# Sums of squares in the second cross-attention: from four columns to one row that a transfer spreads over the partitions

## The chip, the cores and the metric

The kernel runs on one core of one Trainium2 chip. The metric is the device time of one launch in microseconds; the kernel before takes 1813.54 us (median of three runs, 1813.4 to 1814.91).

## The reference

Four layers follow one another on x (8 x 256 tokens of 512 features), each added to x: a cross-attention, a feed-forward layer with ternary weights, a second cross-attention, and a mixture of experts. The change touches the second attention alone:

```
q = layernorm(x) @ Wq + bq        # 16 heads of 128
k, v = ctx @ Wk + bk, ctx @ Wv + bv   # 4 heads of 128, each serves 4 query heads
q = q * rsqrt(mean(q*q over the 128 of a head) + 1e-6) * qn_w     # RMS norm; k likewise
probs = softmax(q @ k.T / sqrt(128) + mask)
x = x + (probs @ v) @ Wo
```

For every token and head the kernel thus needs the sum of the squares of 128 values of q.

## The kernel before, in words

The program is written engine by engine, in an order set by hand; semaphores alone tie the engines together. Matrices in 32-bit precision are kept as two parts, `hi` and `lo`, and `matmul3` (L74 to L80) multiplies them with three matmuls.

The second attention (`ffn0_attention1`) works through 64 units, u = 0 to 63. A unit is one head for two of the eight batches (C = 512 tokens, CT = 4 tiles of 128). Four units (HG = 4) make a block; after the fourth, TensorE runs `project` (48 matmuls of 512 columns) for the four heads together, so each block has three short rounds and one long. There are four groups of query heads (G = 4) of 16 units each.

A query tile stands transposed: the head's 128 values on the partitions, the 512 tokens along the free axis. The steps of unit u, with the engine of each:

- `queries` (TensorE, 12 matmuls of 512 columns) gives q in one of two PSUM banks. ScalarE squares it into `sq` (L1360) and copies it into `q.hi` (L1361); VectorE writes `q.lo` (L1515).
- `square_sums` (TensorE, L1718): for each of the 4 tiles one matmul in full 32-bit precision, with the squares as the weights at rest and a column of ones moving. Its result stands as 128 x 4, a token on each partition. VectorE adds epsilon (L1520), GpSimd raises to the power -1/2 (L1224, `rstd`) and gives `rq`.
- `scores` (TensorE, 12 matmuls of 256 columns); VectorE scales them by `rq` and adds the mask (L1528), takes the negated maxima (L1535, `maxima`); ScalarE takes the exponentials (L1367, `exp`); VectorE divides (L1540, L1544, `normalise`).
- `transposed` (TensorE, L1750), split by ScalarE (L1373) and VectorE (L1549); `output` (TensorE, 12 matmuls of 256 columns on V), split by ScalarE (L1379) and VectorE (L1554).

The loop is a pipeline. In round u TensorE runs `transposed(u)`, `square_sums(u + 2)`, `queries(u + 3)`, `scores(u + 2)`, `output(u)` and, each fourth time, `project`. In the first round of a block `square_sums` stands ahead of `transposed`. In the first rounds of every second block ScalarE and GpSimd also split the next 2048-column weight tile (`wo_hi` and `wo_lo`, or `wq_hi` L1333 and `wq_lo` L1228), and in each block a key and a value tile (L1346 and L1241, L1351 and L1245).

Of the kernel before, what the change touches and what calls it, by code (L numbers as in the profile page):

```python
# [1010 lines left out]
def ffn0_attention1(nc, banks, X, eps, ident, ones, limit, W, keep, prep, stored, rstd, x1T_dram, ahead, first, wq1,  # L1011
# [24 lines left out]
    with Phase(nc) as ctx:  # L1036
# [20 lines left out]
        q = [over.pair(f"a1_q{j}", [P, C]) for j in range(2)]  # L1057
        sq = [over.take(f"a1_sq{j}", [P, C]) for j in range(2)]
# [10 lines left out]
        ssq = sb("ssq", [P, HG, CT])  # L1069
# [44 lines left out]
        s_sq, s_ssq, s_ssqc, s_rq = sema("q_squared"), sema("q_sum"), sema("q_sum_copied"), sema("q_rstd")  # L1114
# [322 lines left out]
        def _(dve):
# [185 lines left out]
            queries(2, 2)
            square_sums(1, 1)
# [29 lines left out]
        def _(pe):  # L1654
# [99 lines left out]
            def output(u):  # L1754
# [7 lines left out]
                for b in range(NB):  # L1762
# [1128 lines left out]
```

## Time and profile before

| | |
|---|---|
| median of three runs | 1813.54 us |
| the profiled execution | 1817.25 us, span 1815.5 us |
| granted TensorE clock | 0.985 of 2.4 GHz over the span |
| the 64 rounds of the second attention | from 651.0 us to about 1291 us |
| busy share of the span | PE 96%, DVE 67%, ACT 47%, POOL 32% |

PE is TensorE, DVE is VectorE, ACT is ScalarE, POOL is GpSimd, SP is SyncE. Times are counted from the first instruction of the span. Instructions of one engine overlap by some tens of nanoseconds, so the step from one start to the next is shorter than the duration that a row gives; an end of a matmul is modelled.

### The profile page before, as it was taken

The numbers are of one execution on the slowest core, as the hardware profiler recorded it, in microseconds if no ns is written. First come the engines' busy times: TensorE is split into PE (matmuls) and PEld (weight loads), VectorE is DVE, ScalarE is ACT, GpSimd is POOL, SyncE is SP. The second block draws the span as 40 slices with busy tenths as digits, with TensorE's granted clock in tenths as the row PEclk, the third lists the DMA queues.
The fourth block names the chain that finished last, engine by engine and source line by source line (L and its number), as shares of the span: only waits on it lengthen the run. The fifth ranks groups of instructions, "written<-read, shape, count | busy, mean of one in ns | idle before, by whom it ended". The sixth has DMA issues, their size and how long they took to land. (4 is left out here: it accounts for less than half of the span.)

```text
span 1815.5 us, 26738 instructions
## 1 busy us (share of the span) xinstructions
PE 1740.2 (96%) x9946; PEld 1443.8 (80%) x9966; DVE 1213.7 (67%) x2313; ACT 851.2 (47%) x1624; POOL 583.5 (32%) x441
## 2 busy tenths in 40 slices
PE   7999998996999989999999999999799999999998
PEld 6998997773444578888888888888667799999876
DVE  5444442895888777767777777777657567676555
ACT  4443432654565564445555555544341256566411
POOL 3111143224686531212132121211110245555342
PEclk9999998998999999999999999999899999999999
DMA  8323211853233761212232221110161488898573
GB/s 313 94 81 105 70 48 33 304 203 99 59 72 91 176 211 59 82 58 82 71 119 73 76 82 59 59 59 1 40 255 49 156 266 273 266 293 258 199 243 110
DMA packets 166346, 238.12 MB, mean 131 GB/s; under 512 B 42054, under 2 KB 103238, under 8 KB 164038
## 3 DMA queue, kind: packets, MB, share of 16 engines
q1 hardware_dynamic: 156620, 203.14, 34.4%
q0 software_dynamic: 9600, 33.30, 5.9%
q8 instruction: 80, 1.31, 0.3%
q14 instruction: 46, 0.38, 0.1%
HBM read 184.24 MB, written 43.78 MB: 126 GB/s over the span
## 5 line engine op out<-in xcount | busy, mean ns | idle before, releaser
L1224 POOL TENSOR_TENSOR a_rq<-a_ssq,a_qhalf 128x4 f32<-128x4 f32 x64 | 65.1, 1017 | 404.7 <-DVE a_ssq L1520 404.7
L1373 ACT ACTIVATE a_pT_hi<-bank 128x512 fp32r<-128x512 f32 x128 | 69.5, 599 | 186.1 <-PE bank L1750 185.9
L78 PE MATMUL bank<-a_xT_hi,a_wq_lo 128*128 128x512 f32 (+1 forms) x384 | 143.9, 375 | 1.4 <-DVE a_xT_lo L503 1.4
L1367 ACT ACTIVATE a_scores<-a_scores,a_nmax 128x256 f32<-128x256 f32 x256 | 127.2, 503 | 27.4 <-DVE a_nmax L1535 27.3
L80 PE MATMUL bank<-a_xT_hi,a_wq_hi 128*128 128x512 f32 (+1 forms) x384 | 138.3, 360 | 0.0
L79 PE MATMUL bank<-a_xT_lo,a_wq_hi 128*128 128x512 f32 (+1 forms) x384 | 138.1, 360 | 0.0
L78 PE MATMUL bank<-a_wo_hi,a_oT_lo 128*128 128x512 f32 x320 | 126.8, 396 | 2.9 <-DVE a_oT_lo L552 1.3
L2059 POOL TENSOR_TENSOR e_wg_lo<-raw_g,e_wg_hi 128x1408 fp32r<-128x1408 f32 x26 | 91.2, 3508 | 112.9 <-ACT e_wg_hi L2126 112.9
L1528 DVE SCALAR_TENSOR_TENSOR a_scores<-bank,a_rq,a_mask 128x256 f32<-128x256 f32 x256 | 106.1, 477 | 28.7 <-PE bank L80 20.4
L79 PE MATMUL bank<-a_wo_lo,a_oT_hi 128*128 128x512 f32 x320 | 124.9, 390 | 0.0
L80 PE MATMUL bank<-a_wo_hi,a_oT_hi 128*128 128x512 f32 x320 | 124.9, 390 | 0.0
L78 PE MATMUL bank<-a_pT_hi,a_V_lo 128*128 128x256 f32 x384 | 111.1, 289 | 8.1 <-DVE a_pT_lo L1549 6.3
L1260 POOL TENSOR_TENSOR f_h<-f_vv,f_gs 128x512 f32<-128x512 f32 x64 | 93.3, 1461 | 62.5 <-DVE f_vv L1465 61.8
L1560 DVE TENSOR_TENSOR X<-X,bank 128x512 f32<-128x512 f32 x64 | 43.8, 687 | 101.4 <-PE bank L80 101.4
L79 PE MATMUL bank<-a_pT_lo,a_V_hi 128*128 128x256 f32 x384 | 110.2, 287 | 0.0
L80 PE MATMUL bank<-a_pT_hi,a_V_hi 128*128 128x256 f32 x384 | 110.1, 287 | 0.0
L1549 DVE TENSOR_TENSOR a_pT_lo<-bank,a_pT_hi 128x512 fp32r<-128x512 f32 x128 | 82.1, 682 | 18.0 <-ACT a_pT_hi L1373 17.9
L1544 DVE TENSOR_SCALAR a_scores<-a_scores,a_rden 128x256 f32<-128x256 f32 x256 | 85.9, 399 | 2.3
L78 PEld LDWEIGHTS bank<-a_pT_hi,a_V_lo 128*128 128x128 f32 x384 | 75.1, 196 | 10.0 <-DVE a_oT_lo L1554 6.9
L80 PEld LDWEIGHTS bank<-a_xT_hi,a_wq_hi 128*128 128x128 f32 x384 | 73.7, 192 | 11.1
L78 PEld LDWEIGHTS bank<-a_xT_hi,a_wq_lo 128*128 128x128 f32 x384 | 74.1, 193 | 10.3 <-DVE a_xT_lo L503 1.8
L1535 DVE TENSOR_REDUCE a_nmax<-a_scores 128x2 f32<-128x512 f32 x128 | 81.2, 675 | 0.0
(416 smaller groups left out, 5326.2 us busy)
## 6 DMA issues: line engine op xcount, KB each, us to landing
raw_g<-in_egw SPq DMA_DIRECT2D x26, 704.0 KB, 4.7
raw_u<-in_euw SPq DMA_DIRECT2D x26, 704.0 KB, 6.2
a_xT_hi<-x1T_hi SPq DMA_DIRECT2D x16, 1024.0 KB, 6.1
a_xT_lo<-x1T_lo SPq DMA_DIRECT2D x16, 1024.0 KB, 8.5
raw_d<-in_edw SPq DMA_DIRECT2D x26, 512.0 KB, 5.9
y_routed<-m_y SPq DMA_DIRECT2D x39, 256.0 KB, 6.3
raw_d<-in_edw SPq DMA_DIRECT2D x26, 192.0 KB, 6.8
a_cTraw<-in_ctxT SPq DMA_DIRECT2D x8, 512.0 KB, 6.0
```

The lines of the kernel that those rows point to most:

```text
L78: pe.matmul(out, w[1], x[0], start=first, stop=False)
L79: pe.matmul(out, w[0], x[1], start=False, stop=False)
L80: return pe.matmul(out, w[0], x[0], start=False, stop=last)
L1224: pool.tensor_tensor(rq[:, h % HG, :], ssq[:, h % HG, :], qhalf[:], ALU.pow).then_inc(s_rq, 1)
L1260: pool.tensor_tensor(h[n % 2][:, j * 512:(j + 1) * 512], vv[u % 2][:], gs[u % 2][:], ALU.mult).then_inc(s_h, 1)
L1367: act.activation(row, row, ACT.Exp, bias=nmax[:, i % 2, t:t + 1], accum_out=den[:, i % 2, t:t + 1]).then_inc(s_exp, 1)
L1373: act.activation(pT[b].hi[:], ptb[b][:].rearrange("p (k s) -> p k s", k=QT), ACT.Copy).then_inc(ft.hi, 1)
L1528: dve.scalar_tensor_tensor(sc[i % 2][:, r, :], scb[b][:, t * S:(t + 1) * S], rq[:, i % HG, r:r + 1], mask[:, t, :], ALU.mult, ALU.add).the ...
L1535: dve.tensor_reduce(nmax[:, i % 2, b * QT:(b + 1) * QT], sc[i % 2][:, b * QT:(b + 1) * QT, :], AX.X, ALU.max, negate=True).then_inc(s_nmax, 1)
L1544: dve.tensor_scalar(row, row, rden[:, i % 2, t:t + 1], None, ALU.mult).then_inc(s_p, 1)
L1549: dve.tensor_tensor(pT[b].lo[:], ptb[b][:].rearrange("p (k s) -> p k s", k=QT), f32(pT[b].hi[:]), ALU.subtract).then_inc(ft.lo, 1)
L2059: pool.tensor_tensor(pairs[w % 2].g.lo[:], raws[raw_of(w)].g[:], f32(pairs[w % 2].g.hi[:]), ALU.subtract).then_inc(s_glo, 1)
```

## The change

Squares get the treatment of the other operands: `sq_hi` is a rounded copy of `sq` (ScalarE), `sq_lo` is the rest (VectorE). Now the ones rest in the array, as a single column `ones_r`, and the squares move, in two matmuls of 512 columns that add up in PSUM. The result is one row of 512 sums on partition 0. ScalarE copies that row to SBUF, adding epsilon and putting the four tiles' values of each token place side by side, and issues a transfer from its own queue that lays the row out as 128 x 4. GpSimd waits for that transfer.

The places in the order change with it. On TensorE `square_sums(u + 3)` now stands in round u between the two halves of `output(u)`, one unit further ahead than before. VectorE does `queries(u + 3)` and the new `squares(u + 3)` ahead of `scores(u + 2)`. ScalarE does `square_sums(u + 3)` (row copy and transfer) late in round u, ahead of its `output(u)`. The prologue is rearranged alike.

```diff
@@ scalar
             def queries(u, g, i, begin=False):
                 act.wait_ge(fq.mm, u + 1)
-                if not begin:
-                    act.wait_ge(s_ssq, u - 1)
...
+                after(act, s_ssq, u - 1)
                 act.activation(sq[i % 2][:], qb[i % 2][:], ACT.Square, bias=b).then_inc(s_sq, 1)
                 act.activation(q[i % 2].hi[:], qb[i % 2][:], ACT.Identity, bias=b).then_inc(fq.hi, 1)
+                after(act, s_ssq, u)
+                act.wait_ge(s_sq, u + 1)
+                act.activation(sq_hi[:], sq[i % 2][:], ACT.Copy).then_inc(s_sqhi, 1)
+
+            def square_sums(u):
+                act.wait_ge(s_ssq, u + 1)
+                if u:
+                    act.wait_ge(s_col[(u - 1) % 2], (u - 1) // 2 * 16 + 16)
+                act.activation(sum_row[0:1, :].rearrange("a (p t) -> a t p", t=CT),
+                               ssb[0:1, :].rearrange("a (t p) -> a t p", t=CT), ACT.Identity,
+                               bias=sum_eps[0:1, :]).then_inc(s_row, 1)
+                act.wait_ge(s_row, u + 1)
+                after(act, s_rq, u - 1)
+                act.dma_start(ssq[u % 2][:], sum_row[0:1, :].rearrange("a (p t) -> a p t", t=CT)).then_inc(s_col[u % 2], 16)
...
+                if u + 3 < G * U:
+                    square_sums(u + 3)
                 output(u, n, i)
@@ gpsimd
-                pool.wait_ge(s_ssqc, u + 1)
-                pool.tensor_tensor(rq[:, h % HG, :], ssq[:, h % HG, :], qhalf[:], ALU.pow).then_inc(s_rq, 1)
+                pool.wait_ge(s_col[u % 2], u // 2 * 16 + 16)
+                pool.tensor_tensor(rq[:, h % HG, :], ssq[u % 2][:], qhalf[:], ALU.pow).then_inc(s_rq, 1)
@@ vector
-            def square_sums(u, i):
-                dve.wait_ge(s_ssq, u + 1)
-                dve.tensor_scalar(ssq[:, i % HG, :], ssb[:, 0:CT], HD * RMS_EPS, None, ALU.add).then_inc(s_ssqc, 1)
+            def squares(u, i):
+                dve.wait_ge(s_sqhi, u + 1)
+                dve.tensor_tensor(sq_lo[i % 2][:], sq[i % 2][:], f32(sq_hi[:]), ALU.subtract).then_inc(s_sqlo, 1)
...
-                if u + 2 < G * U:
-                    square_sums(u + 2, i + 2)
                 transposed(u)
                 if u + 1 < G * U:
                     normalise(u + 1, i + 1)
+                if u + 3 < G * U:
+                    queries(u + 3, i + 3)
+                    squares(u + 3, i + 3)
                 if u + 2 < G * U:
                     scores(u + 2, i + 2)
-                if u + 3 < G * U:
-                    queries(u + 3, i + 3)
-                if u + 2 < G * U:
                     maxima(u + 2, i + 2)
@@ tensor
             def square_sums(u, i):
-                pe.wait_ge(s_sq, u + 1)
+                pe.wait_ge(s_sqlo, u + 1)
...
-                after(pe, s_ssqc, u)
-                for t in range(CT):
-                    last = pe.matmul(ssb[:, t:t + 1], sq[i % 2][:, t * P:(t + 1) * P], ones[:, 0:1], start=True,
-                                     stop=True)
-                last.then_inc(s_ssq, 1)
+                after(pe, s_row, u)
+                pe.matmul(ssb[0:1, :], ones_r[:], sq_hi[:], start=True, stop=False)
+                pe.matmul(ssb[0:1, :], ones_r[:], sq_lo[i % 2][:], start=False, stop=True).then_inc(s_ssq, 1)
...
-                if i % HG == 0 and u + 2 < G * U:
-                    square_sums(u + 2, i + 2)
                 transposed(u, n, i)
-                if i % HG and u + 2 < G * U:
-                    square_sums(u + 2, i + 2)
                 if u + 3 < G * U:
                     queries(u + 3)
                 if u + 2 < G * U:
                     scores(u + 2)
-                output(u)
+                output(u, range(1))
+                if u + 3 < G * U:
+                    square_sums(u + 3, i + 3)
+                output(u, range(1, NB))
```

TensorE, before, at the turn from one short round to the next (a_pT and a_V are `output`, ident is `transposed`, a_xT and a_wq are `queries`; each L1718 matmul in full 32-bit precision is two on the engine):

```order
L79 MATMUL bank<-a_pT_lo,a_V_hi 128x256
L80 MATMUL bank<-a_pT_hi,a_V_hi 128x256
L1750 MATMUL bank<-ident,a_scores_4403 128x128 x8
L1718 MATMUL bank<-ones,a_sq_4411 128x1 x4
L78 MATMUL bank<-a_xT_hi,a_wq_lo 128x512
```

TensorE, of the change, in the middle of `output(u)`:

```order
L78 MATMUL bank<-a_pT_hi,a_V_lo 128x256
L79 MATMUL bank<-a_pT_lo,a_V_hi 128x256
L80 MATMUL bank<-a_pT_hi,a_V_hi 128x256
L1746 MATMUL bank<-a_sq_hi,a_ones_r 1x512
L1747 MATMUL bank<-a_sq_lo_4410,a_ones_r 1x512
L78 MATMUL bank<-a_pT_hi,a_V_lo 128x256
L79 MATMUL bank<-a_pT_lo,a_V_hi 128x256
```

The sums stand later in the round than the matmuls whose result they square, with 18 matmuls of 256 columns between (12 of `scores`, 6 of `output`); before, a whole `output` and a `transposed` stood between.

VectorE, before, one short round:

```order
L1549 TENSOR_TENSOR a_pT_lo<-bank,a_pT_hi 128x512 x2
L1540 RECIPROCAL a_rden<-a_den 128x4
L1544 TENSOR_SCALAR a_scores_4402<-a_scores_4402,a_rden 128x256 x4
L1528 SCALAR_TENSOR_TENSOR a_scores_4403<-bank,a_rq,a_mask 128x256 x4
L1515 SCALAR_TENSOR_TENSOR a_q_lo<-bank,a_bqg,a_q_hi 128x512
L1535 TENSOR_REDUCE a_nmax<-a_scores_4403 128x2 x2
L1554 TENSOR_TENSOR a_oT_lo<-bank,a_oT_hi 128x512
```

VectorE, of the change, the same stretch:

```order
L1578 TENSOR_TENSOR a_pT_lo<-bank,a_pT_hi 128x512 x2
L1569 RECIPROCAL a_rden<-a_den 128x4
L1573 TENSOR_SCALAR a_scores_4402<-a_scores_4402,a_rden 128x256 x4
L1544 SCALAR_TENSOR_TENSOR a_q_lo<-bank,a_bqg,a_q_hi 128x512
L1549 TENSOR_TENSOR a_sq_lo_4410<-a_sq_4412,a_sq_hi 128x512
L1557 SCALAR_TENSOR_TENSOR a_scores_4403<-bank,a_rq,a_mask 128x256 x4
L1564 TENSOR_REDUCE a_nmax<-a_scores_4403 128x2 x2
```

`q_lo` and the new `sq_lo` now stand ahead of the scores.

ScalarE, of the change, one short round (before, L1372, L1378 and the DMA were not there):

```order
L1395 ACTIVATE a_pT_hi<-bank 128x512 x2
L1389 ACTIVATE a_scores_4403,a_den<-a_scores_4403,a_nmax 128x256 x4
L1368 ACTIVATE a_sq_4413<-bank,a_bqg 128x512
L1369 ACTIVATE a_q_hi<-bank,a_bqg 128x512
L1372 ACTIVATE a_sq_hi<-a_sq_4413 128x512
L1355 ACTIVATE a_K_hi<-ahead_ctx 128x512
L1378 ACTIVATE a_sum_row<-bank,a_sum_eps 1x4x128
L1383 DMA a_ssq_4428<-a_sum_row 128x1x4
L1401 ACTIVATE a_oT_hi<-bank 128x512
```

The row copy, which waits for TensorE's sums, and the transfer stand ahead of `a_oT_hi` and of everything of the next round.

## Rows read from the trace of the kernel before

**Rows 1.** The page, part 1: engine, busy us (share of the span), instructions.
```profile
PE 1740.2 (96%) x9946; PEld 1443.8 (80%) x9966; DVE 1213.7 (67%) x2313; ACT 851.2 (47%) x1624; POOL 583.5 (32%) x441
```
**Rows 2.** Windows of two blocks: length, busy by engine, PE clock, DMA.
```profile
900.12:941.33 41.21, 41.05 (x258) 36.55 (x257) 31.18 (x68) 22.12 (x56) 12.04 (x8) 1.00 0.27 90
941.33:982.38 41.05, 40.95 (x257) 36.51 (x256) 29.39 (x68) 20.72 (x54) 6.62 (x6) 1.00 0.19 65
```
**Rows 3.** Timeline of TensorE, first rounds of a block: start us, duration us, instruction.
```profile
941.33 1.09 PE L1750 MATMUL bank<-ident,a_scores 128*128 128x128 f32 x8
942.17 0.48 PE L78 MATMUL bank<-a_xT_hi,a_wq_lo 128*128 128x512 f32 x1
...
944.79 0.39 PE L80 MATMUL bank<-a_xT_hi,a_wq_hi 128*128 128x512 f32 x1
...
947.16 0.28 PE L78 MATMUL bank<-a_pT_hi,a_V_lo 128*128 128x256 f32 x1
...
947.89 1.03 PE L1750 MATMUL bank<-ident,a_scores 128*128 128x128 f32 x8
...
955.31 0.38 PE L1750 MATMUL bank<-ident,a_scores 128*128 128x128 f32 x2
```
**Rows 4.** Timeline of ScalarE in the same round.
```profile
942.99 0.51 ACT L1367 ACTIVATE a_scores<-a_scores,a_nmax 128x256 f32<-128x256 f32 x1
943.48 0.51 ACT L1367 ACTIVATE a_scores<-a_scores,a_nmax 128x256 f32<-128x256 f32 x1
...
945.21 0.69 ACT L1360 ACTIVATE a_sq<-bank,a_bqg 128x512 f32<-128x512 f32 x1 [0.15 <-PE bank L80]
945.80 0.68 ACT L1361 ACTIVATE a_q_hi<-bank,a_bqg 128x512 fp32r<-128x512 f32 x1
946.37 0.63 ACT L1346 ACTIVATE a_K_hi<-ahead_ctx 128x512 fp32r<-128x512 f32 x1
948.09 0.60 ACT L1379 ACTIVATE a_oT_hi<-bank 128x512 fp32r<-128x512 f32 x1 [1.08 <-PE bank L80]
948.58 1.08 ACT L1373 ACTIVATE a_pT_hi<-bank 128x512 fp32r<-128x512 f32 x2
```
**Rows 5.** Timeline of VectorE in the same round.
```profile
948.29 0.74 DVE L1515 SCALAR_TENSOR_TENSOR a_q_lo<-bank,a_bqg,a_q_hi 128x512 fp32r<-128x512 f32 x1
948.95 1.26 DVE L1535 TENSOR_REDUCE a_nmax<-a_scores 128x2 f32<-128x512 f32 x2
```
**Rows 6.** Single lines of the kernel: duration ns min/median/max, first and last start.
```profile
L486 DVE TENSOR_TENSOR a_wq_lo<-a_wraw,a_wq_hi x4: 682/684/686, 9.5 to 13.6; 128x512 fp32r<-128x512 f32 x4
L2151 ACT ACTIVATE r_lg<-bank x4: 586/586/587, 1320.8 to 1356.4; 16x512 f32<-16x512 f32 x4
L1224 POOL TENSOR_TENSOR a_rq<-a_ssq,a_qhalf x64: 1007/1008/1106, 637.7 to 1280.2; 128x4 f32<-128x4 f32 x64
L2587 PE MATMUL bank<-r_xT_lo,r_rw x16: 387/396/632, 1317.6 to 1356.0; 128*8 128x512 f32 x16
L1190 SPq DMA_DIRECT2D a_xT_lo<-x1T_lo x14: 627/632/1257, 657.8 to 1192.3; - x14
```
**Rows 7.** Timeline of SyncE's queue: start, issue duration.
```profile
1317.08 0.32 SPq L2023 DMA_DIRECT2D xT_hi<-r_xT_hi  x1
```
**Rows 8.** Transfers: KB each, us from issue to landing.
```profile
r_gbias<-in_egb SPq DMA_DIRECT2D x1, 3.0 KB, 2.6
a_xT_lo<-x1T_lo SPq DMA_DIRECT2D x16, 1024.0 KB, 8.5
```
**Rows 9.** Timeline of ScalarE, GpSimd, VectorE in a block with a weight tile.
```profile
905.18 1.92 ACT L1333 ACTIVATE a_wq_hi<-ahead_raw 128x2048 fp32r<-128x2048 f32 x1
907.18 4.62 POOL L1228 TENSOR_TENSOR a_wq_lo<-ahead_raw,a_wq_hi 128x2048 fp32r<-128x2048 f32 x1 [5.77 <-ACT a_wq_hi L1333]
912.92 1.30 POOL L1241 TENSOR_TENSOR a_K_lo<-ahead_ctx,a_K_hi 128x512 fp32r<-128x512 f32 x1
911.37 3.02 DVE L1544 TENSOR_SCALAR a_scores<-a_scores,a_rden 128x256 f32<-128x256 f32 x4
```

More of the change, by code:

```diff
@@ L1057, in ffn0_attention1 @@
         q = [over.pair(f"a1_q{j}", [P, C]) for j in range(2)]
+        sq_lo = Region(nc, over.offset)
+        sq_lo = [sq_lo.take(f"a1_sq_lo{j}", [P, C], F32R) for j in range(2)]
         sq = [over.take(f"a1_sq{j}", [P, C]) for j in range(2)]
@@ L1068, in ffn0_attention1 @@
         bqg = [first.bqg, sb("bqg", [P, HG])]
-        ssq = sb("ssq", [P, HG, CT])
+        ones_r, sum_eps = sb("ones_r", [P, 1], F32R), sb("sum_eps", [P, 1])
+        ssq = [sb(f"ssq{j}", [P, CT]) for j in range(2)]
         qhalf = sb("qhalf", [P, CT])
@@ L1086, in ffn0_attention1 @@
         wraw, xT, mask, bq = ahead.raw, first.xT, first.mask, first.bq
+        over = Region(nc, keep.gate_area)
+        sq_hi, sum_row = over.take("a1_sq_hi", [P, C], F32R), over.take("a1_sum_row", [P, C])
+        assert over.offset <= keep.gate_area + 2 * H
         gb, vb, x1b, fob, xb = banks[0:2], banks[2:4], banks[5], banks[4:8:2], banks[7][:].bitcast(BF16)
@@ L1113, in ffn0_attention1 @@
         fq, ft, fo = (Flow(ctx, nc, "a1_" + n) for n in ("q", "pT", "oT"))
-        s_sq, s_ssq, s_ssqc, s_rq = sema("q_squared"), sema("q_sum"), sema("q_sum_copied"), sema("q_rstd")
+        s_sq, s_sqhi, s_sqlo, s_ssq, s_row, s_rq = (sema(n) for n in (
+            "q_squared", "q_squared_hi", "q_squared_lo", "q_sum", "q_sum_row", "q_rstd"))
+        s_col = [sema(f"q_sum_column{j}") for j in range(2)]
         s_sc, s_masked, s_nmax, s_exp, s_rden, s_p = (sema(n) for n in (
@@ L1245, in values_lo @@
                 pool.tensor_tensor(V[n % 2].lo[:], first.Vraw, f32(V[n % 2].hi[:]), ALU.subtract).then_inc(s_vlo, 1)
+            pool.memset(sum_eps[:], HD * RMS_EPS).then_inc(s_const, 1)
             pool.memset(qhalf[:], -0.5).then_inc(s_const, 1)
             pool.memset(last.mhalf[:], -0.5).then_inc(s_lhalf, 1)
-            pool.wait_ge(s_const, 1)
+            pool.wait_ge(s_const, 2)
             pool.wait_ge(s_lhalf, 1)
@@ L1406, in _ @@
             next_norm(T - 4)
+            act.wait_ge(s_const, 2)
+            act.activation(ones_r[:], ones[:, 0:1], ACT.Copy).then_inc(s_const, 1)
             queries(0, 0, 0, True)
@@ L1409, in _ @@
             next_norm(T - 3)
+            square_sums(0)
             queries(1, 0, 1, True)
             next_hi(T - 3)
+            next_norm(T - 2)
+            square_sums(1)
             exp(0, 0)
-            next_norm(T - 2)
             queries(2, 0, 2)
@@ L1416, in _ @@
             next_norm(T - 1)
+            square_sums(2)
             next_hi(T - 1)
@@ L1611, in _ @@
             queries(0, 0)
+            squares(0, 0)
             next_lo(T - 4)
@@ L1614, in _ @@
             queries(1, 1)
+            squares(1, 1)
             ffn_add(T - 1)
@@ L1617, in _ @@
             next_mean(T - 1)
-            square_sums(0, 0)
+            next_lo(T - 3)
+            next_shift(T - 2)
             scores(0, 0)
             maxima(0, 0)
-            next_lo(T - 3)
-            next_shift(T - 2)
             queries(2, 2)
-            square_sums(1, 1)
+            squares(2, 2)
             next_lo(T - 2)
@@ L1752, in transposed, with output @@
                     last.then_inc(ft.mm, 1)
-            def output(u):
+            def output(u, halves):
                 i, n = u % U, u // HG
@@ L1761, in output @@
                 after(pe, fo.lo, u)
-                for b in range(NB):
+                for b in halves:
                     pe.wait_ge(ft.lo, u * NB + b + 1)
@@ L1766, in output @@
                                        part(pT[b], slice(None), k), k == 0, k == QT - 1)
-                last.then_inc(fo.mm, 1)
+                if NB - 1 in halves:
+                    last.then_inc(fo.mm, 1)
             def project(u, n):
@@ L1799, in _ @@
             queries(1, True)
+            square_sums(0, 0)
             down(T - 1)
-            square_sums(0, 0)
+            square_sums(1, 1)
             next_xT(T - 3)
@@ L1804, in _ @@
             queries(2)
-            square_sums(1, 1)
             next_xT(T - 2)
             scores(1)
+            square_sums(2, 2)
             next_xT(T - 1)
@@ L2794, in program @@
             keep.base = nc.sbuf_base
+            keep.gate_area = keep.base - 2 * H
             xT = [None, next_pair("a1_xT1", [P, KD, C], 1)]
```

1 line of the change is left out of this document (added).

## The prediction

> **What bounds the kernel now.** I read the page first: TensorE is busy 96% of the span [rows 1]. Then windows over two blocks of the second attention, cut where TensorE starts a block: 41.21 and 41.05 us long, TensorE busy for 41.05 and 40.95, VectorE for 31.2 and 29.4, ScalarE for 22.1 and 20.7, the clock at its upper level [rows 2]. TensorE idles for about 0.1 us in a block, so there is no slack in which a new wait on it could vanish: what it saves is gained in full and what it waits is lost in full. That holds only while the others keep up, so the timelines of the three engines in one round come next, to see when each result that the change makes TensorE wait for could be there.
>
> I count from 941.33, the start of a block's first round [rows 3]. TensorE starts its first query matmul at +0.84; the last starts at +3.46 and ends at +3.85; the second half of output(u) starts at +5.83, and the round is over at +6.56. This round holds no square sums (they stand ahead of it). The next one holds them and is 955.31 - 947.89 = 7.42 long, so the sums of one unit cost 0.86.
>
> **What TensorE saves.** The new sums are two matmuls of 512 moving columns with one column at rest. The steps of the queries give the price: 11 steps in 944.79 - 942.17 = 2.62, that is 0.24 each [rows 3]. That few resting columns make no odds is seen where eight rest: 387 to 396 ns for 512 columns, as the 390 of a query matmul [rows 3, 6]. So 0.47 in place of 0.86: 0.39 saved per unit, 64 x 0.39 = 25.0 us.
>
> **What TensorE waits.** The sums of u + 3 stand after the first half of output(u), thus at +5.83. They need sq_lo, and that has a chain behind it which starts when the last query matmul ends, at +3.85: ScalarE starts the squares at +3.88 and q_hi at +4.47, which ends at +5.15 [rows 4]; sq_hi follows at +5.04 and takes about what the copy in its place takes now (0.63, to +5.67), so it is not what is late. VectorE starts q_lo 0.04 after q_hi's end, at +5.19; a follower of it starts 0.66 later [rows 5], sq_lo at +5.85. A subtraction of two SBUF tiles of this shape takes 0.684 [rows 6]: +6.53, and with 0.04 for the semaphore TensorE goes on at +6.57. It wanted to at +5.83: a wait of 0.74. Nothing can shorten this in the first round of a block, where the other engines have caught up behind the projection. It is more than the 0.39 saved.
>
> In the rounds after, the chain is longer, since ScalarE has a loop. From the start of a unit's sums: both matmuls done +0.63 (0.24 + 0.39); semaphore 0.04; the row copy, one partition of 512 elements, which I take at the 0.59 of a 16-partition copy out of PSUM [rows 6]: +1.26; semaphore +1.30; the transfer's issue, d; then a_oT_hi 0.49, two pT_hi at 0.49, four exponentials at 0.49 with their accumulator reads (the step from 942.99 to 943.48), the squares 0.59, and q_hi to its end 0.68 [rows 4]: 1.30 + d + 0.49 + 0.98 + 1.96 + 0.59 + 0.68 = 6.00 + d; then as above 0.04, q_lo 0.66, sq_lo 0.68, semaphore 0.04: 7.42 + d from sums to sums. TensorE's own work in that time is 6.56 + 0.47 = 7.03. The wait is thus 0.39 + d, and at least 0.74. The key and value copies (0.57) don't lengthen the loop: they stand where ScalarE waits for the sums.
>
> The trace has no transfer issued by ScalarE. SyncE's take from 0.32 [rows 7] over 0.63 in the median to 1.26 [rows 6]. I take 0.5, since most stand at 0.3 to 0.65: a wait of 0.89. The Trainium skill (DMA: Bandwidth & Descriptors, Anatomy of one DMA — SWDGE (gpsimd) path) puts a sequencer's dispatch at about 50 ns, for GpSimd's kind of transfer; the issue rows here are six times that and more. By the page's figure every wait would be at its floor of 0.74, and the sum about 7 us lower.
>
> The loop issues sums for 61 units (three belong to the prologue): 16 first rounds at 0.74 = 11.8 and 45 others at 0.89 = 40.1, together 51.9 us.
>
> **Blocks with a weight tile.** In seven blocks (four wo tiles, three wq) the first round has ScalarE round a tile for 1.92, from 905.18 to 907.10 [rows 9]. Now sq_hi stands ahead of it and the row copy behind it: tile, bias and key copies end at about +8.0, while the sums are ready for the row copy at 6.57 + 0.67 = +7.2. The loop starts about 0.75 late, and TensorE waits that longer. Besides, four divisions of VectorE took 3.02 and ended at 914.39, just behind GpSimd's a_K_lo (912.92 + 1.30 = 914.22) [rows 9]; such a block has 1.8 more of VectorE's time than the other kind [rows 2]. Now TensorE pays nothing for that; after the change q_lo and sq_lo stand behind those divisions and TensorE behind sq_lo. So between 0.75 and 2.6 in each; I take 1.5, less than the middle, as the collision needs GpSimd to hit the same instructions: 7 x 1.5 = 10.5 us. The Trainium skill (SBUF — State Buffer, SBUF: two separate sides) says that a VectorE operation with two SBUF inputs and a GpSimd one that reads SBUF exclude each other for the whole instruction. The 3.02 agrees with such a lock; sq_lo has two SBUF inputs and so could be held up too, by the rule for up to 4.62 in a block. In my times it lies 1 us or more clear of GpSimd's long operation.
>
> **What stays hidden.** A transfer of 3 KB lands 2.6 after its issue [rows 8], which I take for this one of 2 KB; GpSimd's power takes 1.0 [rows 6]. So rq is there 1.8 + 2.6 + 1.1 = 5.5 after the sums began, and VectorE asks for it at 7.9: 2.4 to spare. VectorE gains 0.60 and loses 0.07 in a round; its 29.4 to 31.2 of 41 become 31.5 to 33.3, which is no bound. The epsilon add on VectorE goes off a path that was not limiting. The prologue has TensorE idle around these sums anyway, and its end hangs on layer norm copies: 0, give or take 2.
>
> **The sum.** -25.0 + 51.9 + 10.5 = +37.4 on the profiled execution of 1817.25 (span 1815.5): 1854.7. That execution is 3.7 over the median of the runs, so the median becomes 1813.5 + 37.4 = 1851.
>
> Ends: with d = 0.32 all waits at 0.74 (45.1) and 0.75 in seven blocks, +25, 1839. If sq_lo lands 0.08 earlier and the tiles cost nothing, 61 x 0.66 - 25.0 = +15, 1829. With d = 1.26 the 45 waits are 1.65: 86.1 - 25.0 + 7 x 2.6 = +79, 1893.
>
> **The rivals.** (1) Faster: the squares are ready when TensorE comes to them. The matmuls between the queries' end and the sums last 1.98 and the chain must then fit in; with no wait at all the 25 us of the saving remain: 1788. Point of decision: a wait under 0.39 per unit. For it stands only that VectorE and ScalarE have spare time overall; against it that each of the five steps has its own row, and that they sum to 2.7. 0.06; a wait near 0.39, no change, 0.04.
> (2) The row's transfer is late. The large loads of x take 8.5 to land [rows 8] and one starts in most blocks; if the little transfer queues behind it for, say, 8, rq comes 3 after VectorE asks, of which 1 is spare before the exponentials start: 2 x 14 blocks = +28 more, 1879. Against: it is 128 tiny pieces on another queue. 0.08.
> (3) An issue from ScalarE costs as SyncE's longest: 1893 with all its company, about 1882 with the tile blocks at 1.5. 0.08.
> My forecast, a wait at its 0.74 to 1.0: 0.74. Less than 0.2% (3.6 us) either way can't be told from no change here. Only rival 1 gives faster, 0.06; same 0.04; slower 0.90. Range 1829 to 1883: it leaves out rival 1, no change, and half of rival 3.
>
> **What would show it.** Right: TensorE idle before L1746 (the first of the two sums) for 0.7 to 1.0 in each round, released by VectorE's sq_lo L1549; two matmuls at 0.24 steps there; a plain block about 43 long in place of 41.05; ScalarE waiting for TensorE before L1378; rq waiting for nothing but its transfer, some 2 to 3 after issue; VectorE's scores not waiting for rq. Wrong: no idle before L1746 (rival 1), scores released by GpSimd's L1232 in most rounds (rival 2), a gap of over 1 between L1378 and the next ScalarE instruction (rival 3), or the sums' matmuls far from 0.24.

## The result and the profile after

The changed kernel takes 1915.3 us (median of 4 runs, 1909.47 to 1916.69) where the kernel before takes 1814.22 beside it (1813.4 to 1815.51): slower by 5.5%, ratio 1.0549 with a 95% interval of 1.0535 to 1.0564. The prediction was 1851, range 1829 to 1883. Its sign held and the two waits that it named were found; their sizes, and a third wait that it did not have, put the time outside the range: the profiled span went from 1815.5 to 1914.8, +99.3, where +37.4 was forecast. Of the kernels below, one of the four runs of E6 took 2857 us at a granted clock of 0.556 and is left out of its median and ratio.

Page, part 1, of after (answers to [rows 1]), and windows of two blocks of after, one without and one with a weight tile (columns as in [rows 2], which they answer to):

```profile
PE 1738.9 (91%) x9562; PEld 1411.3 (74%) x9582; DVE 1249.9 (65%) x2313; ACT 953.1 (50%) x1753; POOL 586.3 (31%) x442
```
```profile
990.58:1036.56 45.98, 39.96 (x232) 33.70 (x233) 31.78 (x68) 26.81 (x62) 7.02 (x6) 1.00 0.18 58
845.39:895.01 49.62, 42.27 (x233) 35.66 (x233) 33.52 (x68) 28.69 (x63) 12.02 (x8) 0.93 0.23 75
```

A plain block (one without a weight tile) took 41.05 before and one with a tile 41.21. In the plain block TensorE now works 1.0 us less than before (39.96 against 40.95) and idles 6.0, where it idled 0.1; in the other it is busy 1.2 longer, part of it at a lower clock, and idles 7.4. The 64 rounds, from the start of the first to that of the last, grew from 639.1 to 734.2: +95.1 of the +99.3. What stands ahead of them grew by 2.0, what follows by 2.2.

TensorE of after, first two rounds of the plain block that starts at T = 990.58 (answers to [rows 3]):

```profile
990.58 1.09 PE L1777 MATMUL bank<-ident,a_scores 128*128 128x128 f32 x8 [0.78 <-DVE X L1589]
...
997.17 0.40 PE L1746 MATMUL bank<-a_sq_hi,a_ones_r 128*1 128x512 f32 x1 [0.60 <-DVE a_sq_lo L1549]
...
997.40 0.40 PE L1747 MATMUL bank<-a_sq_lo,a_ones_r 128*1 128x512 f32 x1
...
998.35 1.03 PE L1777 MATMUL bank<-ident,a_scores 128*128 128x128 f32 x8
...
1005.86 0.39 PE L1746 MATMUL bank<-a_sq_hi,a_ones_r 128*1 128x512 f32 x1 [1.54 <-DVE a_sq_lo L1549]
```

ScalarE (answers to [rows 4]) and VectorE (to [rows 5]) of after in the same rounds:

```profile
994.46 0.69 ACT L1368 ACTIVATE a_sq<-bank,a_bqg 128x512 f32<-128x512 f32 x1 [0.16 <-PE bank L80]
995.05 0.68 ACT L1369 ACTIVATE a_q_hi<-bank,a_bqg 128x512 fp32r<-128x512 f32 x1
995.62 0.63 ACT L1372 ACTIVATE a_sq_hi<-a_sq 128x512 fp32r<-128x512 f32 x1
...
997.84 1.19 ACT L1378 ACTIVATE a_sum_row<-bank,a_sum_eps 1x512 f32<-1x512 f32 x1 [1.07 <-PE bank L1747]
...
999.05 0.48 ACTq L1383 DMA_DIRECT2D a_ssq<-a_sum_row  x1
...
999.63 0.60 ACT L1401 ACTIVATE a_oT_hi<-bank 128x512 fp32r<-128x512 f32 x1 [0.61 <-ACT a_sum_row L1378]
...
1003.04 0.69 ACT L1368 ACTIVATE a_sq<-bank,a_bqg 128x512 f32<-128x512 f32 x1
```
```profile
995.77 0.75 DVE L1544 SCALAR_TENSOR_TENSOR a_q_lo<-bank,a_bqg,a_q_hi 128x512 fp32r<-128x512 f32 x1
...
996.43 0.68 DVE L1549 TENSOR_TENSOR a_sq_lo<-a_sq,a_sq_hi 128x512 fp32r<-128x512 f32 x1
...
1004.46 0.75 DVE L1544 SCALAR_TENSOR_TENSOR a_q_lo<-bank,a_bqg,a_q_hi 128x512 fp32r<-128x512 f32 x1
...
1005.12 0.68 DVE L1549 TENSOR_TENSOR a_sq_lo<-a_sq,a_sq_hi 128x512 fp32r<-128x512 f32 x1
```

The first round is 998.35 - 990.58 = 7.77, which is 6.56 + 0.47 + 0.74 as forecast, with the sums at +6.59. From these sums to the next, though, is 1005.86 - 997.17 = 8.69, not 7.92. Step by step: the row copy starts at +0.67 (as forecast) and takes 1.21 to the transfer's issue (forecast 0.63 with its semaphore); the issue 0.58 to the next instruction (0.50); `a_oT_hi` to the next squares 3.41 (3.43); those to `q_lo` 1.42 (1.31); `sq_lo` 0.66 later, TensorE 0.74 behind that (0.72). Of the 0.77 too much 0.58 is the row copy. And the first line of TensorE's rows holds a wait that the forecast doesn't have: the block begins 0.78 late, behind VectorE's last add of the projection (L1589).

Waits of after, 640 to 1400 us (engine, line, waited for, us in total, times, longest), and its single lines L1378 and L1383, the latter also to landing:

```profile
POOL a_rq L1232 <- DMA a_ssq<-a_sum_row: 363.6, 58, 19.8
PE bank L1746 <- DVE a_sq_lo L1549: 90.4, 62, 4.1
ACT a_sum_row L1378 <- PE bank L1747: 88.8, 54, 3.1
```
```profile
L1378 ACT ACTIVATE a_sum_row<-bank,a_sum_eps x64: 1146/1191/1220, 632.6 to 1373.0; 1x512 f32<-1x512 f32 x64
```
```profile
L1383 ACTq DMA_DIRECT2D a_ssq<-a_sum_row x64: 477/477/545, 633.8 to 1374.2; - x64
...
DMA to landing us min/median/max: 1.9/2.0/6.1
```

Last the block with a weight tile: its rounds are 7.81, 11.80, 9.12 and 20.88, where the plain block's are 7.77, 8.70, 8.64 and 20.87. ScalarE, GpSimd, VectorE and TensorE in it (answers to [rows 9]):

```profile
851.00 1.91 ACT L1350 ACTIVATE a_wo_hi<-ahead_raw 128x2048 fp32r<-128x2048 f32 x1
...
853.32 1.18 ACT L1378 ACTIVATE a_sum_row<-bank,a_sum_eps 1x512 f32<-1x512 f32 x1
...
858.88 2.09 DVE L1573 TENSOR_SCALAR a_scores<-a_scores,a_rden 128x256 f32<-128x256 f32 x4
...
861.05 1.25 POOL L1253 TENSOR_TENSOR a_V_lo<-ahead_ctx,a_V_hi 128x512 fp32r<-128x512 f32 x1
861.55 1.31 DVE L1549 TENSOR_TENSOR a_sq_lo<-a_sq,a_sq_hi 128x512 fp32r<-128x512 f32 x1
...
862.91 0.59 PE L1746 MATMUL bank<-a_sq_hi,a_ones_r 128*1 128x512 f32 x1 [3.76 <-DVE a_sq_lo L1549]
```
```profile
858.00:862.00 4.00, 1.15 (x10) 0.95 (x8) 3.30 (x7) 2.82 (x8) 3.97 (x4) 0.89 0.58 197
862.00:866.00 4.00, 3.09 (x13) 2.69 (x14) 3.61 (x7) 1.49 (x2) 0.30 (x1) 0.50 0.59 200
866.00:870.00 4.00, 4.00 (x17) 3.38 (x16) 2.36 (x5) 3.35 (x11) 1.01 (x1) 0.76 0.02 1
```

`sq_lo` takes 1.31 instead of 0.68 and ends 0.56 behind GpSimd's `a_V_lo`; TensorE waits 3.76, from 859.15 to 862.91. The granted clock falls to 0.50, the lower level of 1.2 GHz, within that wait and stays there for the whole second window (the 0.89 and the 0.76 beside it are means over both levels). Between 650 and 1420 us after has nine stretches at the lower level, 64.9 us together, before four of 27.3.

Not every such wait was followed by the lower level. In the block that starts at T = 1132.21 TensorE waits as long:

```profile
1149.70 0.40 PE L1746 MATMUL bank<-a_sq_hi,a_ones_r 128*1 128x512 f32 x1 [3.74 <-DVE a_sq_lo L1549]
```
```profile
1132.21:1180.39 48.18, 39.94 (x232) 33.70 (x232) 33.25 (x68) 28.60 (x64) 11.99 (x8) 1.00 0.23 77
```

Its clock stays at 1.00, and it takes 48.18, which is 2.2 over a plain block, where four blocks with the lower level take 3.6 to 3.75 more than one.

### The profile page after: what moved, and what is told of

Its sections match the earlier page's. It is cut to its first block and busy times, and to the rows that moved or that the text cites. A ratio compares the mean times of both kernels' runs of the same rounds, so it can differ in the third digit from the quotient of the medians.

```text
span 1914.8 us, 26420 instructions
## 1 busy us (share of the span) xinstructions
PE 1738.9 (91%) x9562; PEld 1411.3 (74%) x9582; DVE 1249.9 (65%) x2313; ACT 953.1 (50%) x1753; POOL 586.3 (31%) x442
## 5 line engine op out<-in xcount | busy, mean ns | idle before, releaser
L1378 ACT ACTIVATE a_sum_row<-bank,a_sum_eps 1x512 f32<-1x512 f32 x64 | 76.2, 1190 | 88.8 <-PE bank L1747 88.8
L1589 DVE TENSOR_TENSOR X<-X,bank 128x512 f32<-128x512 f32 x64 | 43.7, 687 | 111.4 <-PE bank L80 111.4
L1269 POOL TENSOR_TENSOR f_h<-f_vv,f_gs 128x512 f32<-128x512 f32 x64 | 93.2, 1460 | 62.5 <-DVE f_vv L1494 61.8
L1746 PE MATMUL bank<-a_sq_hi,a_ones_r 128*1 128x512 f32 x64 | 25.9, 405 | 91.5 <-DVE a_sq_lo L1549 91.5
L1777 PE MATMUL bank<-ident,a_scores 128*128 128x128 f32 x512 | 74.4, 293 | 14.3 <-DVE X L1589 11.7
```

What stands on the lines that cost most here:

```text
L1269: pool.tensor_tensor(h[n % 2][:, j * 512:(j + 1) * 512], vv[u % 2][:], gs[u % 2][:], ALU.mult).then_inc(s_h, 1)
L1378: act.activation(sum_row[0:1, :].rearrange("a (p t) -> a t p", t=CT), ssb[0:1, :].rearrange("a (t p) -> a t p", t=CT), ACT.Identity, bias= ...
L1777: last = pe.transpose(ptb[b][:, k * S + t * P:k * S + (t + 1) * P], sc[i % 2][:, r, k * P:(k + 1) * P], ident[:])
```

## The experiments

All times are medians, and the kernel before took 1813.24 to 1813.85 beside those of E1 to E12. "Rounds" are the four of an undisturbed block without a weight tile, first to last, from one start of `transposed` to the next.

| kernel | us | against before (95%) | rounds | such a block |
|---|---|---|---|---|
| before | 1814.22 | | 6.56, 7.42, 7.4, 19.7 | 41.05 |
| after | 1915.3 | 1.0535 to 1.0564 | 7.77, 8.70, 8.64, 20.87 | 45.98 |
| E1 | 1901.59 | 1.0467 to 1.0502 | 7.77, 8.18, 8.12, 20.37 | 44.44 |
| E2 | 1898.8 | 1.0451 to 1.0496 | 7.77, 8.18, 8.12, 20.37 | 44.44 |
| E3 | 1898.86 | 1.0453 to 1.0488 | 7.06, 8.68, 8.64, 20.87 | 45.25 |
| E4 | 1895.44 | 1.0431 to 1.0470 | 8.37, 8.68, 8.65, 19.1 | 44.78 |
| E5 | 1905.13 | 1.0486 to 1.0527 | as after | 46.0 |
| E6 | 1845.62 | 1.0156 to 1.0206 | 6.56, 6.99, 6.98, 19.6 | 40.12 |
| E7 | 1903.79 | 1.0476 to 1.0511 | 7.86, 8.27, 8.21, 20.45 | 44.78 |
| E8 | 1828.08 | 1.0055 to 1.0093 | 7.45, 7.41, 7.40, 19.66 | 41.92 |
| E9 | 1814.86 | 0.9993 to 1.0014 | 6.56, 6.76, 6.84, 19.01 | 39.17 |
| E10 | 1810.61 | 0.9969 to 0.9991 | 6.78, 6.74, 6.74, 18.99 | 39.25 |
| E11 | 1833.21 | 1.0070 to 1.0110 | as E6 | 40.3 to 41.0 |
| E12 | 1805.75 | 0.9936 to 0.9968 | as E9 | 39.1 |

### E1, E2 and E7: the row copy

E1 writes the row in one run and leaves the tokens in the order of the tiles:

```diff
-                act.activation(sum_row[0:1, :].rearrange("a (p t) -> a t p", t=CT),
-                               ssb[0:1, :].rearrange("a (t p) -> a t p", t=CT), ACT.Identity,
-                               bias=sum_eps[0:1, :]).then_inc(s_row, 1)
+                act.activation(sum_row[0:1, :], ssb[0:1, :], ACT.Identity, bias=sum_eps[0:1, :]).then_inc(s_row, 1)
```

> The row copy writes its 512 values one behind the other, the transfer is the same; so the four sums of a token are not those of its four tiles, and the output is another. Theory A (ScalarE's loop of 8.69 us from sums to sums sets the rounds, and 0.6 of it is the price of writing in steps of 16 bytes): the copy takes 0.59 in place of 1.19, short rounds behind the first of a block go from 8.7 to 8.1, 45 x 0.6 = 27 us less, 1888 us (1883 to 1893). Theory B (the row costs 1.19 because a single partition is slow to copy): no change. Theory C (the transfer's landing sets the rounds): no change.

E2 keeps the order of after, and puts the steps on the side that is read (512 bytes apart in PSUM):

```diff
-                act.activation(sum_row[0:1, :].rearrange("a (p t) -> a t p", t=CT),
-                               ssb[0:1, :].rearrange("a (t p) -> a t p", t=CT), ACT.Identity,
+                act.activation(sum_row[0:1, :].rearrange("a (p t) -> a p t", t=CT),
+                               ssb[0:1, :].rearrange("a (t p) -> a p t", t=CT), ACT.Identity,
```

> The copy walks the tokens, reads PSUM in steps of 128 values and writes in one run. If only a write in steps is slow: 0.59 for the copy and 27 us less than the changed kernel, 1888 us. If a read in steps is as slow: 1.19 and 1915 us.

E7 copies as E1 and lets the matmuls read the squares in that order:

```diff
-                pe.matmul(ssb[0:1, :], ones_r[:], sq_hi[:], start=True, stop=False)
-                pe.matmul(ssb[0:1, :], ones_r[:], sq_lo[i % 2][:], start=False, stop=True).then_inc(s_ssq, 1)
+                turned = lambda x: x.rearrange("k (t p) -> k p t", t=CT)
+                pe.matmul(ssb[0:1, :], ones_r[:], turned(sq_hi[:]), start=True, stop=False)
+                pe.matmul(ssb[0:1, :], ones_r[:], turned(sq_lo[i % 2][:]), start=False, stop=True).then_inc(s_ssq, 1)
```

> The sums' matmuls read the squares in steps of 128 values, so that the row comes out in the right order and the copy runs through. If the matmul's step stays at 0.23: as e1, 1888 us. If a moving operand read in steps of 512 bytes is slower, say twice, two matmuls cost 0.46 more in each of 61 rounds: 1888 + 28 = 1916.

The row copy in E2, and the first matmul of the sums in E7 and in after, as single lines:

```profile
L1378 ACT ACTIVATE a_sum_row<-bank,a_sum_eps x64: 657/679/682, 628.7 to 1355.2; 1x512 f32<-1x512 f32 x64
```
```profile
L1745 PE MATMUL bank<-a_sq_hi,a_ones_r x64: 432/433/588, 631.5 to 1363.9; 128*1 128x512 f32 x64
```
```profile
L1746 PE MATMUL bank<-a_sq_hi,a_ones_r x64: 386/397/587, 631.9 to 1372.3; 128*1 128x512 f32 x64
```

The copy falls from 1.19 to 0.68, whether its read is in one run (E1, median 680 ns) or in steps (E2, 679). So the stepped write alone costs the 0.51, and each round behind it is 0.51 shorter (8.69 to 8.18): one for one on TensorE. The Trainium skill (SBUF — State Buffer, Door 1: The DMA port swizzle) says that each access to a new 16-byte line of SBUF pays a penalty. The write of after, in steps of 16 bytes, agrees with that. The same paragraph says that non-contiguous PSUM access slows matmuls; for ScalarE's read of PSUM no run here shows a cost, and the matmuls of E7 read their squares from SBUF. In E7 the stepped read costs 36 ns in a matmul and 0.09 in a round, far from twice the time, and the kernel came out between its two forecasts (1903.79).

The forecast for E1 and E2 was 27 us less, and they came out 13.7 and 16.5 less. The plain block gained 1.54, which over 15 blocks would be 23, but blocks with a weight tile gained next to nothing: six of the seven stayed at 49 to 50 us, as their second round grew from 11.8 to 12.7 in most of them, and the lower clock came in ten stretches of 61.4 us together.

### E3 and E4: another place for the sums

E3 puts them behind the whole `output(u)`:

```diff
-                output(u, range(1))
+                output(u, range(NB))
                 if u + 3 < G * U:
                     square_sums(u + 3, i + 3)
-                output(u, range(1, NB))
```

> The sums behind both halves of the output. Theory A (a chain that starts at the queries' end in a block's first round, then a loop of 8.69 on ScalarE): the first round's wait of 0.7 is filled by the second half, the loop of the others is as long as before, so a block gains 0.71 once: 16 x 0.71 = 11 us less, 1904 (1900 to 1908). Rival (each round's wait stands by itself and 0.71 of it is filled each time): 61 x 0.71 = 43 less, 1872.

The first round lost its wait (7.77 to 7.06), the other three none (8.70 to 8.68, 8.64, 20.87): they are held by the ring through ScalarE, from sums to sums, which TensorE's place for them doesn't shorten. E3 is 16.4 under after where 11 was forecast (range 1900 to 1908, measured 1898.86): the seven blocks with a tile came down by 8.4 together, and 7 x 0.71 is 5.0. E4 moves only the long round's sums, behind `project`, on TensorE and ScalarE:

```diff
@@ scalar
+                late = i % HG == HG - 1
-                if u + 3 < G * U:
+                if u + 3 < G * U and not late:
                     square_sums(u + 3)
                 output(u, n, i)
+                if u + 3 < G * U and late:
+                    square_sums(u + 3)
@@ tensor
+                late = i % HG == HG - 1
-                if u + 3 < G * U:
+                if u + 3 < G * U and not late:
...
+                if u + 3 < G * U and late:
+                    square_sums(u + 3, i + 3)
```

> In the long round the sums stand behind the projection (ScalarE: the row copy behind a_oT_hi). Theory A: the wait in that round (1.6) is filled by 11 us of matmuls, and the sums then cover the 0.78 that the next transposes wait for the last add of VectorE: 15 x 2.4 = 36 us less than the changed kernel, 1879 (1874 to 1886). Rival (the add's wait only moves to the sums, since they too come too early): 15 x 1.6 = 24 less, 1891.

The long round fell by 1.77 (20.87 to 19.1), as the wait in it went. The next round rose by 0.60, because its row copy now starts when that round does. The wait for VectorE's add fell from 11.7 to 4.8 us over 15 blocks. So the exchange nets 1.2 in a plain block, and the result, 1895, lies above both forecasts.

### E5: blocks with a weight tile

The wq tiles' rounding goes from the block's first round to its long one:

```diff
-                if i == U // 2 and g + 1 < G:
+                if i == U // 2 + HG - 1 and g + 1 < G:
```

> The three wq tiles are rounded and subtracted in the long round of their block, under the projection, in place of its first round. If the tile in the first round is what makes such a block 49.6 in place of 46.0, with a wait of 3.8 for sq_lo and a half clock behind it: 3 x 3.5 = 10 us less, 1905, and no half clock in those three blocks. If something else of those blocks does it: 1915.

The three blocks fell from 49.7, 49.6 and 48.2 to 46.1, as plain ones, and the two of them that had a stretch at the lower clock have none any more (seven stretches with 47.8 us remain, of nine with 64.9). The kernel took 1905.13, as forecast. A window of E5 over the second of them shows the clock whole and GpSimd as busy as in any block with a tile:

```profile
932.94:979.00 46.06, 39.95 (x232) 33.67 (x232) 31.90 (x68) 28.64 (x64) 12.15 (x8) 1.00 0.25 81
```

So the surcharge of such a block, 2.2 to 3.7, hangs on when the tile is rounded, not on the work itself.

### E6, E8 and E11: the form of the sums apart from their place

E6 has the row and both parts, copied as in E2, with `square_sums(u + 2)` in the old places on TensorE and ScalarE:

```diff
@@ scalar, tensor
+                if i % HG == 0 and u + 2 < G * U:
+                    square_sums(u + 2)
                 transposed(u)
+                if i % HG and u + 2 < G * U:
+                    square_sums(u + 2)
...
-                if u + 3 < G * U:
-                    square_sums(u + 3)
```

> The row form (with the quicker copy that gathers from PSUM) in the place of the kernel before: sums of u + 2 beside the transposes of u, on ScalarE too. The squares are then a round old, so no wait of TensorE's. Theory A: only the saving of 0.39 to 0.40 per unit is left, and nothing else is late: 1814 - 25 = 1789 (1787 to 1798). Rival (the row's way over ScalarE, the transfer of 2.0 and GpSimd makes rq late: sums end +1.5, copy to +2.4, issue, landing +4.9, power +6.0, scores wanted at +5.4 by VectorE): rounds grow by some 0.6 behind VectorE, 45 x 0.6 = 27 more, 1816.

E8 is the kernel before, columns and all, with TensorE's sums in the new place:

```diff
-                if i % HG == 0 and u + 2 < G * U:
-                    square_sums(u + 2, i + 2)
                 transposed(u, n, i)
-                if i % HG and u + 2 < G * U:
-                    square_sums(u + 2, i + 2)
...
-                output(u)
+                output(u, range(1))
+                if u + 3 < G * U:
+                    square_sums(u + 3, i + 3)
+                output(u, range(1, NB))
```

> The kernel before with the place alone changed: the four column sums of u + 3 between the halves of output(u), no sq_hi and sq_lo. They need the squares alone, done at +4.6 and wanted at +5.8: no wait. What remains is that the transposes of a block's first round wait about 0.8 for the last add, which the sums covered: 15 x 0.8 = 12 us more than before, 1826 (1820 to 1832). If the place costs nothing by itself: 1814.

TensorE of E8 in a plain block:

```profile
945.52 1.09 PE L1750 MATMUL bank<-ident,a_scores 128*128 128x128 f32 x8 [0.78 <-DVE X L1560]
...
952.97 1.03 PE L1750 MATMUL bank<-ident,a_scores 128*128 128x128 f32 x8
```

E8's other rounds are those of before; its first is 0.03 longer than the 7.42 of a round with sums, and before that round TensorE waits 0.78 for the add. That wait is the plain block's +0.87: the old sums ahead of the first `transposed` took 0.86 and hid it. Over 15 blocks it is 11.7 us, and the kernel is 14.6 slower, where 12 were forecast. This term belongs to the place alone.

E6's shortest plain block is 40.12, against before's 41.05; others take 40.3 to 41.7, and the last two 42.8 and 42.7. So with the old places two parts and a row would pay at best, by 0.93 of the 1.56 that four times 0.39 promise. VectorE of E6 in two of its short rounds:

```profile
960.70 0.68 DVE L1584 TENSOR_TENSOR a_oT_lo<-bank,a_oT_hi 128x512 fp32r<-128x512 f32 x1
...
964.20 0.75 DVE L1545 SCALAR_TENSOR_TENSOR a_q_lo<-bank,a_bqg,a_q_hi 128x512 fp32r<-128x512 f32 x1
964.86 0.68 DVE L1550 TENSOR_TENSOR a_sq_lo<-a_sq,a_sq_hi 128x512 fp32r<-128x512 f32 x1
...
965.61 1.66 DVE L1558 SCALAR_TENSOR_TENSOR a_scores<-bank,a_rq,a_mask 128x256 f32<-128x256 f32 x4
...
968.37 0.68 DVE L1584 TENSOR_TENSOR a_oT_lo<-bank,a_oT_hi 128x512 fp32r<-128x512 f32 x1
```
```profile
957.96:971.93 13.97, 13.97 (x94) 12.49 (x93) 13.49 (x32) 12.24 (x31) 4.65 (x4) 1.00 0.49 167
```

VectorE is busy for 13.49 of 13.97 us in these two rounds, ScalarE for 12.24. VectorE has next to nothing to spare, and where GpSimd's tiles slow it, TensorE waits: 15.1 us for its divisions and 9.2 for `sq_lo` between 640 and 1400. E6's blocks with a tile take 43.7 to 46.7 and are together 26 us longer than before's, of the 32 by which the total is over before. Both forecasts were missed. That of 1789 fell by these blocks, and the rival's 1816, a late `rq`, was not the cause either: VectorE waited 4.8 us for `rq` in five times, and 6.4 in eight before. E11 is E6 with E5's edit.

> The two-part row in the old place, and the three wq tiles in the long round. If the tile in the first round makes those blocks 45 in place of 41, with waits for sq_lo and a half clock: 3 x 4 = 12 less than e6, 1834. If not: 1847.

It got 12.4 us of the 32 back, as forecast (12); its three wq blocks take 40.35 to 41.5.

### E9, E10 and E12: one part

E9 is E6 with the squares written once, rounded (`sq` as F32R), `sq_hi` and `sq_lo` and the second matmul left out, so that the low part of the squares is missing from the sums:

```diff
-                pe.matmul(ssb[0:1, :], ones_r[:], sq_hi[:], start=True, stop=False)
-                pe.matmul(ssb[0:1, :], ones_r[:], sq_lo[i % 2][:], start=False, stop=True).then_inc(s_ssq, 1)
+                pe.matmul(ssb[0:1, :], ones_r[:], sq[i % 2][:], start=True, stop=True).then_inc(s_ssq, 1)
```

> The squares are written once, already rounded, and the row is summed by one matmul: no sq_hi, no sq_lo, no second matmul; place as in the kernel before, the copy that gathers. The low part of the squares is left out of the sum. TensorE pays 0.23 in place of 0.86 per unit, 64 x 0.63 = 40 less than before. Theory A (all the loss came from the chain over q_hi, q_lo and sq_lo and from ScalarE's loop through it): 1774 (1772 to 1790, the upper end if blocks with a weight tile keep some of their waits). Rival (the row's way, copy, transfer and GpSimd, costs as such): 1800 or more.

E10 is the same with the places of after (its row copy stays E2's quicker one).

> The same one-part squares in the new place, between the halves of output(u); the low part is left out of the sum. They need the squares alone, at +4.6 for +5.8: no wait of TensorE's; ScalarE's loop from sums to sums is 5.8 and no bound. Theory A: 1814 - 40 and 15 x 0.86 for the transposes that wait for the last add: 1787 (1782 to 1797). Rival (the row copy on ScalarE between the sums and a_oT_hi is what holds the rounds): rounds stay above 7.4, 1830 or more.

E12 is E9 with E5's edit.

> One-part squares in the old place and the wq tiles in the long round; the low part is left out of the sum. If blocks with a tile still lose 1 to 3 us in e9: 3 to 8 less than e9. If one-part squares leave VectorE room to take the collision with GpSimd, as the kernel before had: the same as e9 within 2 us.

Undisturbed blocks are 39.1 to 39.25 in all three, 1.9 under before. E10 has after's order, with the quicker row copy, and yet no wait worth the name for its sums (2.1 us in four times): rounds of 6.74. So ScalarE's row copy, transfer and place don't hold a round above 7.4 by themselves; what after waits for is the way over `q_hi`, `q_lo` and `sq_lo` behind the squares.

Of 1.9 times 16, some 30 us, E9 keeps nothing, E10 3 and E12 8. E9 and E10 thus missed their 1774 and 1787 by 41 and 24, and E9's rival, that the row's way costs as such, had the nearer number (1800 or more). In E12 the 64 rounds took 623.7 where before took 639.1, thus 15.4 less: the four blocks with a wo tile take 43.4, 40.3, 42.1 and 39.2, other blocks up to 40.4, and the last two full ones 41.9 and 40.6, where before's took 41.1 and 40.9. Between 640 and 1400 VectorE waited 13.4 us for `rq` in E12 (9.4 in E9, 6.4 before), and TensorE 11.2 for `pT_lo` (6.3 before). So the row's way takes a part; no run gives it apart from the rest. Two more places are seen where gain goes. GpSimd, VectorE and TensorE of E12 in a block with a wo tile:

```profile
982.76 4.42 DVE L1564 TENSOR_SCALAR a_scores<-a_scores,a_rden 128x256 f32<-128x256 f32 x4
...
983.18 1.29 POOL L1246 TENSOR_TENSOR a_K_lo<-ahead_ctx,a_K_hi 128x512 fp32r<-128x512 f32 x1
...
985.51 1.25 POOL L1250 TENSOR_TENSOR a_V_lo<-ahead_ctx,a_V_hi 128x512 fp32r<-128x512 f32 x1
```
```profile
984.69 0.70 PE L1763 MATMUL bank<-ident,a_scores 128*128 128x128 f32 x4 [0.86 <-DVE a_scores L1564]
...
986.97 0.70 PE L1763 MATMUL bank<-ident,a_scores 128*128 128x128 f32 x4 [1.58 <-DVE a_scores L1564]
```

Four divisions that take 1.14 elsewhere take 4.42 beside GpSimd, and TensorE, now earlier at its transposes, waits 2.4 for them. And the stage after the attention is longer in E12, 530.3 us from the last round's start to the end of the span, against 525.3. Windows of its first 20 to 110 us, of E12 and of before:

```profile
1292.60:1342.60 50.00, 41.54 (x195) 29.14 (x196) 29.07 (x47) 18.08 (x30) 11.03 (x5) 0.83 0.61 237
1342.60:1382.60 40.00, 36.11 (x148) 27.61 (x147) 27.03 (x127) 6.73 (x9) 0.00 (x0) 0.91 0.22 80
```
```profile
1310.00:1360.00 50.00, 43.84 (x218) 31.10 (x216) 28.86 (x47) 20.02 (x32) 10.77 (x5) 0.88 0.66 261
1360.00:1400.00 40.00, 36.09 (x150) 27.75 (x150) 29.21 (x136) 5.55 (x8) 0.00 (x0) 0.96 0.17 55
```

The granted clock is 0.05 lower in both. Set matmul against matmul, counted from the last round's start, E12 lies 0.8 behind at 33 us and 2.5 at 56, behind this wait, which was 1.27 before:

```profile
1329.14 0.41 PE L2600 MATMUL bank<-r_xT_hi,r_rw 128*16 128x512 f32 x1 [2.96 <-DVE r_xT_lo L2261]
```

VectorE comes later there because it waits 4.33 for a transfer of `r_xn` to land, and 2.62 before. The other 2.5 of the 5.0 come while the clock is at its lower level: for 3.4 us right behind that wait, where before has no such stretch, and for 6.8 instead of 3.4 some 100 us behind the last round's start. Why the transfer lands later isn't settled. E12 is the fastest kernel of the study, 0.5% under before, at the price of the squares' low part.

## Why the prediction was right in its sign and wrong in its size

- **TensorE's saving, -25.0: right.** The two matmuls step 0.23 to 0.24, and the first round's length comes out to the hundredth.
- **The wait's floor of 0.74 in first rounds, 11.8: right.** The chain of five steps is as worked out.
- **The ring in the other 45 rounds, 40.1: mis-sized, the largest miss.** The step that failed is "the row copy, one partition of 512 elements, which I take at the 0.59 of a 16-partition copy out of PSUM". That row [rows 6] is written in one run; this copy writes in steps of 16 bytes and takes 1.19. Its place among the sums makes it a term for TensorE one for one, as E1 and E2 show. With the issue (0.58 to the next instruction instead of 0.50) and 0.11 more from the squares to `q_lo` the ring is 0.77 longer: 45 x 0.77 = 34.7 missing.
- **The first round's start: missed.** I priced the sums' own wait at the new place and never asked what their old place had covered. A block's last add of VectorE was 0.78 behind TensorE's first transpose, hidden by 0.86 of sums. E8 isolates it: 11.7 us.
- **Blocks with a weight tile, 10.5: half.** My sum had 1.5 for each of the seven. They are longer than plain ones by 3.6 to 3.75 in four of them, 2.2 and 1.3 in the last two and 4.7 in the first, less what they were longer before (2.4 in the first, up to 0.2 in the others): 19.9 us. In the block shown the sums wait 2.2 longer than in a plain round, within my 0.75 to 2.6: ScalarE's row copy starts 0.67 later (7.93 into the block, against 7.26), the divisions gave 0.95 (2.09 against 1.14), `sq_lo` 0.63. I had left `sq_lo` out as 1 us clear of GpSimd; it was hit by the short `a_V_lo`, not the long tile. The Trainium skill (SBUF — State Buffer, SBUF: two separate sides) says that a VectorE operation with two SBUF inputs and a GpSimd operation that reads SBUF take turns, and the one that starts first holds the other up to its end. `a_V_lo` started 0.50 ahead of `sq_lo`, which ended 0.56 behind it: that agrees. The other 1.4 of the 3.6 come with the stretch at the lower clock (0.50) behind the wait, a term that I didn't have: the block from 1132.21, with a wait of 3.74 and the clock at 1.00, is 2.2 longer than a plain one and no more. E5 takes both away together.
- **The sum:** 37.4 + 34.7 + 11.7 + 9.4 = 93.2, against 95.1 measured in the 64 rounds. The prologue gave 2.0, at the end of its 0 plus or minus 2; of the 2.2 behind the last round's start 1.8 are there 18 us later, and in that stretch the clock was at its lower level for 6.3 us, before for 0.6.
- **The rivals fell.** There is no round without the wait (1). The transfer lands 2.0 after its issue, 6.1 at worst, and VectorE waited for `rq` twice, 1.7 us in all (2). The issue takes 0.48 (3), so my 0.5 was right. By its own terms the price of (3) with the tile blocks at 1.5 is 1885 (86.1 - 25.0 + 10.5 over 1813.5), not 1882. That VectorE is no bound held in after, where TensorE waits anyway; in E6, without that wait, VectorE was busy for 97% of two rounds and TensorE waited for its divisions and for `sq_lo` in blocks with a tile.

That the range missed too has more than one reason. Its ends were drawn around the issue's cost, from 0.32 to 1.26, while the row copy, just as unseen in the trace, stood in it with a single value. But that alone doesn't explain it: E1 and E2, with the copy at 0.68, still took 1901.6 and 1898.8, above the 1883. The wait for the late add and the lower clock in blocks with a tile stood in it with nothing.

## What to carry to other kernels

When a loop through several engines sets the pace, each instruction put into it costs the bound engine its full length, as the 0.51 of the row copy did, so give each a low and a high price, the form of its access included, and not only the one that looks strange. When work is moved on a saturated engine, ask what it had hidden where it stood: the old place may have paid for a late neighbour. A small saving on a saturated engine also needs the next engine to have room in the same rounds: VectorE, busy for 78% of a plain block of E6, was busy for 97% of two of its short rounds.

## What the runs showed of the hardware

- ScalarE, one partition of 512 values from PSUM to SBUF: 1.19 us when it writes in steps of 16 bytes, 0.68 in one run, and still 0.68 when only the read is stepped. Sixteen partitions took 0.59 in another stage [rows 6].
- A transfer of 2 KB within SBUF in 128 pieces from ScalarE's queue: 0.48 of ScalarE's time to issue, 2.0 to landing. The 3 KB of [rows 8] took 2.6.
- A moving operand read in steps of 512 bytes: 433 ns instead of 397 for 512 columns.
- Around TensorE's wait of 3.76 (to 862.91) the granted clock fell to 0.50, where it stood from 862 to 866. The waits of 1.5 in plain blocks left it at 1.00, but so did the one of 3.74 that ended at 1149.70, and behind one of 2.18 that ended at 1242.30 it was 0.50 from 1243.4 to 1246.8. In these rows the length of the last wait alone doesn't decide it.
